# Experts' rows written back by token, and read in plain loads, in a windowed-attention, banded-attention and expert block

## Time and profile before

| | us |
|---|---|
| median of three runs | 3094.0 |
| lowest and highest | 3090.27 and 3098.82 |
| span of the profiled execution, first to last instruction | 3088.7 |
| PE busy | 2544.2 |
| DVE busy | 1965.5 |
| ACT busy | 1865.7 |
| POOL busy | 1914.2 |

### The profile page before, as it was taken

How to read it: one execution, slowest core, us unless ns; L and a number is a source line. 1 busy time by engine, 2 the same in 40 slices (tenths; PEclk the granted TensorE clock), 3 DMA queues, 4 the chain that set the end, 5 groups by cost and what they waited for, 6 DMA issues and landing times.

```text
span 3088.7 us, 77036 instructions
## 1 busy us (share of the span) xinstructions
PE 2544.2 (82%) x27338; PEld 1794.8 (58%) x27338; DVE 1965.5 (64%) x5091; ACT 1865.7 (60%) x3409; POOL 1914.2 (62%) x2270
## 2 busy tenths in 40 slices
PE   6898889989888899889988988899888887676830
PEld 3565655556666666666666666666665665554520
DVE  4577777777666666777676676767776765522222
ACT  3666656666767677677776677767777654432310
POOL 1335555555444444576666576666667878779986
PEclk9998888888999999899999999999999988788965
DMA  5223333334445454144333343434343434456743
GB/s 208 104 110 117 117 132 150 147 127 138 147 173 182 161 183 161 60 148 123 100 122 117 107 144 122 126 96 127 119 149 111 131 109 135 123 171 203 244 127 91
DMA packets 262427, 421.99 MB, mean 137 GB/s; under 512 B 41740, under 2 KB 141080, under 8 KB 261280
## 3 DMA queue, kind: packets, MB, share of 16 engines
q1 hardware_dynamic: 219232, 327.69, 31.2%
q0 software_dynamic: 32768, 67.17, 7.7%
q10 hardware_dynamic: 10048, 22.19, 2.2%
HBM read 198.26 MB, written 231.22 MB: 139 GB/s over the span
## 4 chain that ended last, share of the span: by engine, by line
PE 48%; POOL 17%; ACT 15%; issue 10%; DVE 7%; DMA 2%; ACTq 1%; SPq 1%; POOLq 0%; DVEq 0%
PE bank_m L834 7%; POOL yg L1233 7%; PE bank_m L827 4%; PE bank_to L761 4%; POOL x_sorted L1223 4%; PE bank_s L801 4%; PE bank_s L807 3%; PE bank_s L716 3%; ACT pt_sb_a L1051 2%; POOL xin L1243 2%; PE bank_to L770 2%; PE bank_s L729 2%; ACT L1178 2%; ACT v_a L1036 2%; PE bank_s L739 2%
## 5 line engine op out<-in xcount | busy, mean ns | idle before, releaser
L1223 POOL DMA_INDIRECT x_sorted<-xn_c,place_i x512 | 534.3, 1044 | 282.1 <-PE bank_s L700 109.2
L1233 POOL DMA_INDIRECT yg<-y_sorted,place_i x512 | 521.4, 1018 | 241.1 <-PE bank_to L783 107.5
L1216 POOL TENSOR_TENSOR s_sb_a<-s_sb_a,mx_a 128x512 f32<-128x512 f32 x256 | 267.8, 1046 | 587.7 <-DVE mx_a L1607 586.9
L1599 DVE TENSOR_TENSOR s_sb_a<-bank_s,bias_a 128x512 f32<-128x512 f32 x256 | 176.6, 690 | 355.3 <-PE bank_s L700 257.7
L827 PE MATMUL bank_m<-xe,wk_e 128*128 128x512 f32 x552 | 280.5, 634 | 37.7 <-ACT hid L1084 27.7
L834 PE MATMUL bank_m<-wk_e,hid 128*128 128x128 f32 x2208 | 283.3, 291 | 0.9 <-ACT hid L1084 0.9
L834 PEld LDWEIGHTS bank_m<-wk_e,hid 128*128 128x128 f32 x2208 | 277.7, 208 | 2.2 <-issue 1.9
L1216 POOL TENSOR_TENSOR s_sb_b<-s_sb_b,mx_b 128x512 f32<-128x512 f32 x256 | 269.7, 1054 | 11.5 <-DVE mx_b L1607 11.5
L761 PE MATMUL bank_to<-k_consts,p_sb_b 128*128 128x128 f32 x1024 | 179.0, 300 | 92.2 <-ACT pt_sb_a L1051 56.1
L1051 ACT ACTIVATE pt_sb_b<-bank_to 128x512 f32<-128x512 f32 x256 | 152.5, 596 | 146.4 <-PE bank_to L761 145.7
L1207 POOL TENSOR_TENSOR km_a<-qk_a,k_consts 128x128 f32<-128x128 f32 x512 | 215.7, 445 | 40.0 <-DVE qk_a L1451 35.4
(11 more groups left out here) (221 smaller groups left out, 6266.7 us busy)
## 6 DMA issues: line engine op xcount, KB each, us to landing
y_sorted<-t_back SPq DMA_DIRECT2D x192, 512.0 KB, 5.5
y_sorted<-yo SPq DMA_DIRECT2D x170, 256.0 KB
wk_e<-in_w_experts_dram SPq DMA_DIRECT2D x134, 321.0 KB
xs<-x_sorted SPq DMA_DIRECT2D x134, 256.0 KB
t_kept<-t SPq DMA_DIRECT2D x64, 256.0 KB
t_back<-t_kept SPq DMA_DIRECT2D x32, 512.0 KB
xin<-in_x_dram SPq DMA_DIRECT2D x128, 112.0 KB
x_res<-in_x_dram SPq DMA_DIRECT2D x256, 56.0 KB
```

The source lines that it names most:

```text
L1216: pool.tensor_tensor(s[:, :, :], s[:, :, :], m[:, :, None].to_broadcast(shape), ALU.subtract).then_inc(s_sub[w], 1)
L1223: pool.indirect_dma_start(out=x_sorted[group_of[d] % XSIDES].ap(), out_offset=bass.IndirectOffsetOnAxis(ap=place_i[:, d, n:n + 1], axis=0) ...
L1233: pool.indirect_dma_start(out=yg[:, c % 2, n, :], out_offset=None, in_=y_sorted[side].ap(), in_offset=bass.IndirectOffsetOnAxis(ap=place_i ...
L1599: tt(s_sb[0][:, :, :].rearrange("p (r h) n -> p r (h n)", h=2), scores, bias_a[:, kind, :, :].rearrange("p (r h) n -> p r (h n)", h=2), AL ...
```

## The change

**What it does.** Each row that is scattered to `x_sorted` is 130 floats wide now: 128 channels, the row of the output that belongs to the token (`HOME`), and the token's first expert (`FIRST`). When a tile comes back, DVE works out from these two, and from the number of the tile's own expert, which row each output belongs to (`back_to`), and POOL scatters the tile by it to `y_tokens`, with 4 indirect DMAs of 128 rows for each tile (`scatter_back`). The two outputs of a token lie side by side there, so an image's 2048 rows are contiguous, and SP loads them with one plain DMA of 1 MB (in `bring_back`). So `store_pair`, `gather`, `fill` and `apart` are gone, and `scatter_back` is new on POOL. `yo` has three buffers.

The places of the indirect DMAs are written out in two lists, as (step, move place), with steps from 8 on in the next pass: `BACK_AT` for the 8 of each slot's pair, `OUT_AT` for the 16 of an image. A second image is summed in passes 24 to 26 and 29 to 31. For the images of the tail there are four buffers for outputs and residuals, laid over buffers that only the passes need. Several small buffers share memory now, and the constants are split into two inputs.

```diff
-PAUSE = 4
-YSIDES = 3
-UNPAUSED = 4
-FILLS = BUFFER // TOKENS
-FILLS_PER_PASS = 12
+PART = 1
+HOME, FIRST, ROW_W = D, D + 1, D + 2
+YO, MOVES = 3, PART * SUB
+BACK_AT = (((4, 1), (4, 1), (4, 2), (4, 3), (4, 3), (5, 0), (5, 1), (5, 2)),
+           ((6, 1), (6, 2), (6, 3), (7, 1), (7, 2), (7, 3), (8, 0), (8, 1)),
+           ((9, 1), (9, 2), (9, 3), (10, 1), (10, 2), (11, 0), (11, 1), (11, 2)))
+OUT_AT = ((5, 0), (5, 2), (5, 3), (6, 0), (6, 1), (6, 2), (6, 3), (7, 0), (7, 1), (7, 2), (7, 3),
+          (8, 0), (8, 1), (8, 2), (8, 2), (8, 3))
-TWO_SUMS_FROM = 29
-PAIRS_PER_SUM = 2.5
+TWO_SUMS_FROM = 24
+PAIRS_TO_SUM = 3
...
             def bring_back(c):
...
+                sp.dma_start(t2_home[kept].rearrange("p t d -> p (t d)"), t2_kept.ap()[c, :, :]).then_inc(t2_in[kept], 16)
+                after(sp, stored[home], 16 * IO_DMAS * y_uses(c))
+                tiles_landed(sp, last_tile[group_of[c]])
+                first = last_image[group_of[c] - 1] + 1 if group_of[c] else 0
+                at = TOP * (SPARE + TOKENS * (c - first))
+                rows = y_tokens[group_of[c]].ap()[at:at + TOP * TOKENS, :]
+                sp.dma_start(y_home[home].rearrange("p t n d -> p (t n d)"),
+                             rows.rearrange("(p r) d -> p (r d)", p=P)).then_inc(y_in[home], 16)
...
-            def gather(c, n):
-                done, side = last_tile[group_of[c]], group_of[c] % YSIDES
...
+            def scatter_back(u, k):
+
+                _, q, _ = pairs[u].members[k // MOVES]
+                if k % MOVES == 0:
+                    pool.wait_ge(yo_ready, q + 1)
+                j = k % MOVES
+                pool.indirect_dma_start(out=y_tokens[pairs[u].group].ap(),
+                                        out_offset=bass.IndirectOffsetOnAxis(ap=back_to[:, q % YO, j:j + 1], axis=0),
+                                        in_=yo[:, q % YO, j, :], in_offset=None).then_inc(y_out[q % YO], 16)
...
                 def moves(k):
 
+                    for j in (i - 1, i):
+                        at = (t + TILES * (i - j), k)
+                        for slot in range(SLOTS_PER_PASS):
+                            u = slots[j][slot] if 0 <= j < PASSES else None
+                            if u is not None:
+                                for m, when in enumerate(BACK_AT[slot][0:MOVES * len(pairs[u].members)]):
+                                    if when == at:
+                                        scatter_back(u, m)
+                        if on(j - 3):
+                            for row, when in enumerate(OUT_AT):
+                                if when == at:
+                                    scatter(j - 3, row)
...
-            for c in range(first_tail_sum, IMAGES):
-                for k in range(TOP * TILES):
-                    gather(c, k)
-                    if c < IMAGES - UNPAUSED:
-                        apart()
+            for row, (t, _) in enumerate(OUT_AT):
+                if t >= TILES:
+                    scatter(IMAGES - 1, row)
+            for u in tail:
+                for k in range(MOVES * len(pairs[u].members)):
+                    scatter_back(u, k)
...
             def slots_back(q, m, banks):
...
-                after(dve, y_out[q % 2], 16 * (q // 2))
-                tt(yo[:, q % 2, :, :], banks[:, m, :].rearrange("p (j d) -> p j d", j=SUB),
-                   w[:, None, B2_AT:B2_AT + D].to_broadcast([P, SUB, D]), ALU.add).then_inc(yo_ready, 1)
+                after(dve, y_out[q % YO], 16 * MOVES * (q // YO))
+                for h in range(PART):
+                    stt(back_to[:, q % YO, SUB * h:SUB * h + SUB], rows[:, h, :, FIRST], w[:, h, OWN_AT:OWN_AT + 1],
+                        rows[:, h, :, HOME], ALU.not_equal, ALU.add)
+                tt(yo[:, q % YO, :, :].rearrange("p (n j) d -> p n j d", n=PART),
+                   banks[:, m, :].rearrange("p (n j d) -> p n j d", n=PART, j=SUB),
+                   w[:, :, None, B2_AT:B2_AT + D].to_broadcast([P, PART, SUB, D]), ALU.add).then_inc(yo_ready, 1)
```

More of the change, by code:

```diff
@@ L119, in shape_constants @@
     put("base", rows(REGION * e))
+    put("experts", rows(e))
+    put("home", TOP * (SPARE + TILES * ch[:, None] + np.arange(TILES)[None]))
     img = np.zeros((SIDE, SIDE), np.int32)
@@ L576, in _ @@
                     store_image(s)
-                if here[0] is not None:
-                    store_pair(here[0])
                 if first:
@@ L584, in _ @@
                     load_residual(a, 0)
-                if here[1] is not None:
-                    store_pair(here[1])
-                if i >= 0:
-                    for n in range(FILLS_PER_PASS * i, min(FILLS_PER_PASS * (i + 1), YSIDES * FILLS)):
-                        fill(n)
                 following = slots[i + 1][0] if i + 1 < PASSES else None
@@ L826, in hidden @@
                         pe.wait_ge(gelu_ready, CH * q + ch - 1)
-                    mm(banks[:, ch, :], w[:, P * ch:P * ch + P], xe[:, m, :], start=True, stop=True).then_inc(z_ready, 1)
+                    for h in range(PART):
+                        own = slice(SLOTS * h, SLOTS * h + SLOTS)
+                        last = mm(banks[:, ch, own], w[:, h, P * ch:P * ch + P], xe[:, m, own], start=True, stop=True)
+                    last.then_inc(z_ready, 1)
             def expert_out(q, m, end, banks):
@@ L1083, in gelu @@
                     act.wait_ge(z_ready, CH * q + ch + 1)
-                    func(hid[:, CH * m + ch, :], banks[:, ch, :], ACT.Gelu,
-                         bias=w[:, B1_AT + ch:B1_AT + ch + 1]).then_inc(gelu_ready, 1)
+                    for h in range(PART):
+                        own = slice(SLOTS * h, SLOTS * h + SLOTS)
+                        last = func(hid[:, CH * m + ch, own], banks[:, ch, own], ACT.Gelu,
+                                    bias=w[:, h, B1_AT + ch:B1_AT + ch + 1])
+                    last.then_inc(gelu_ready, 1)
             act.preload_act_table_set(EXP_LN_SET)
@@ L1300, in _ @@
                     step(i, t)
-            for k in range(12, TOP * TILES):
-                scatter(IMAGES - 1, k)
-                apart()
-            for c in sums[PASSES - 1][1:]:
-                for k in range(12, TOP * TILES):
-                    gather(c, k)
-                    apart()
-            for c in range(first_tail_sum, IMAGES):
-                for k in range(TOP * TILES):
-                    gather(c, k)
-                    if c < IMAGES - UNPAUSED:
-                        apart()
+            for row, (t, _) in enumerate(OUT_AT):
[4 more added lines that the diff above has]
+                    scatter_back(u, k)
         @block.vector
@@ L1592, in biased @@
+                    tt(rows[:, :, 0, :], rows[:, :, 0, :], t2_home[kept], ALU.add).then_inc(summed, 1)
             def biased(w, n):
```

330 lines of the change are left out of this document (155 added, 175 removed).

## The result

The changed kernel takes 3140.3 us (median of four runs, 3139.3 to 3150.1), the kernel before 3092.1 us beside it. The ratio is 1.0172, with a 95% interval of 1.0129 to 1.0215: 1.7% slower, where 1.1% was forecast. The profiled execution has a span of 3137.6 us; the forecast had 3121.7.

What follows compares the result with a forecast made beforehand. PE was the busiest engine, with POOL's masking holding it up in crowded passes and POOL's gathers setting the end. Span 3088.7 + 97 - 64 = 3121.7 us, plus 5.3 to the median: 3127 us, 1.1% slower; 8 in 10 range 3035 to 3168.

Steps and rivals of the forecast that it cites:

- The passes lose, the tail gains: Whole kernel: pass 33's step 4 comes 97 us later, and the tail from there takes 64 us less.
- the rival in which the passes take the moves in their stride: Passes: PE's late start is partly caught up, 2.5 us lost a pass, 3048 us in all; chance 0.31.
- A crowded step is POOL's: Passes: POOL needs 2.6 + 1.27 n us for a step of n moves, 11.5 in step 6, 12.8 in step 7.
- PE is late, and the light steps don't make it good: Passes without a sum: PE waits for POOL's masked keys and can't catch up; 4.6 us a pass, 32 for seven.
- A sum meets the masking: Nine passes summing an image: DVE's product at step 5 meets POOL's masking; 7.8 us a pass, 70 in all.
- The full clash: Rival: each pass with a sum loses 9.9 us, 3159; with every fourth tail move at 1.91 us, 3209; chance 0.09.
- Passes 17 and 23: No pair in the first slot, so step 4 is light: 5.5 us lost in each, 11 us together.
- The last passes: Passes 29 and 30 become 92.3 us each, -5 together; pass 31 gains 3 us, pass 32 gains 8.
- The tail: From pass 33's step 4, POOL's moves are the bound: 318 us where it was 382, -64 us.
- At nothing: Fills, SP's stores, 1 MB loads and DVE's additions cost or gain nothing; additions, if uncovered, 30 us in all.

Runs made afterwards that it cites:

- e1_out: Changed kernel with one list altered: an image's 16 scatters go out in steps 5 to 7, 0 and 1 instead of 5 to 7 and 0; 3013.9 us.
- e9_behind: Changed kernel, same moves in each step, but in steps 6, 7 and 0 those between subtractions and masking stand behind the masking; 3064.4 us.
- e7_late: Changed kernel with a single sum at step 1 of the next pass instead of at steps 5 and 6; 3108.6 us.
- e8_fills: Changed kernel with the 192 stores of 512 KB of zeros put back into passes 0 to 15; 3142.0 us.
- e12_no_rows: Changed kernel without DVE's computation of the rows: indices filled once ahead of the first pass, scatters and places kept; 3170.7 us.
- e3_home: Changed kernel with DVE's computation of the rows replaced by one operation filling indices from a constant, scatters and places kept; 3135.6 us.

## Why the prediction was right, point by point

- *The passes lose, the tail gains.* By step 4 of pass 33 the kernel is 121.3 us behind where 97 were forecast, and the tail takes 309.7 us where 318 were. Both parts have their sign and nearly their size; the rival in which the passes take the moves in their stride is out, and e1_out shows that it takes one list to make it true.
- *A crowded step is POOL's.* Forecast 11.5 and 12.8 us for the steps 6 and 7, measured 12.26 and 12.85. The 0.8 us more are masking at 1.29 for 0.76 us and a move of 1.25 us, both in step 6. The two subtractions and the masking are 2.86 us by the prediction's own figures and not 2.6; gaps of 0.16 us instead of 0.30 between a move and another operation make up for it.
- *PE is late, and the light steps don't make it good.* Shown by PE's waits of 2.60 and 2.40 us and by e9_behind. Mis-sized is the loss of a pass without a sum: the seven lost 43.0 us together, not 32, 6.1 us each and not 4.6. The clock had been left out, and it is about half of what these passes lost (12.7 of 23.7 us in the passes 11 to 14). What lowers it is not shown: in e1_out step 1 has 0.70 too, without such a wait.
- *A sum meets the masking.* Forecast 7.8 us a pass, measured 82.8 / 9 = 9.2. The 3.2 us put down to the sum were right in size (94.5 for 91.2, and e7_late takes 3.4 away), but not in place: the prediction had the product meet step 5's masking, and that masking ends before the product begins. The product holds up a move, and the additions hold up step 6's masking and the move behind it: 1.4, 1.0 and 0.8 us in pass 20. That the sum comes out at the forecast's is in part luck. What made such a pass longer than forecast is the crowding beneath. The Trainium skill, "SBUF — State Buffer", section "SBUF: two separate sides", made an estimated 9.4 us of such a pass. The measured 9.2 is nearer to it, but not for its reason: it had 4.8 us for the sum, and the sum added 3 to 3.4; no run here shows that POOL was shut out for a whole sum.
- *The full clash* as a rival had 9.9 us for such a pass and was nearly met there, but by the crowding and not by the sum; in the tail it had every fourth move long, and 9 of 201 were.
- *Passes 17 and 23.* Forecast 5.5 us each, measured 8.1 and 13.3. This step failed: no pair in the first slot lightens step 4, but the steps 6 and 7 are as full as in other passes (14.0 and 12.9 us in pass 17, 14.0 and 13.3 in pass 23).
- *The last passes.* 29 and 30 became 95.3 and 98.0 us, not 92.3. Of this, 1.4 us each is what all passes with a sum took over the forecast; the other 1.6 and 4.3 stay open. The second image that they sum does not explain them: the steps 1 and 2, where its sum stands, take 24.2 and 24.1 us together, and 24.1 and 23.9 in the passes 19 and 21, which sum one. 31 and 32 gave back 28 us and not 11. For 31 the prediction misread the kernel before: it had the pauses begin behind that stretch, but the first stands at 2578.2, and 25 of them lie inside (2536.3 to 2626.1). PE's need, from which it took 87 us, was no bound either: PE is busy for 63.9 of the 78.4 us. For 32, 41 moves, seven subtractions and the gaps fit into 64.0 us, since the waits that were put at 13 us are 5.
- *The tail.* It has 201 moves, not 208; at 1.264 us they are 254 us (forecast: 264). Nine long moves add 15.7 (forecast: 20); three waits for tiles add 13, which were not forecast; from the last move's end to the span's are 25.5 us (forecast: 34), because DVE waited 4.8 us for the first of the three last images, and the other two landed beside the sums. The forecast had all three loaded first, 21 us at the tail's mean of 213 GB/s; from 3116 to 3125 us the DMA engines moved 423.
- *At nothing.* The fills, by e8_fills; DVE's additions, though they took 0.68 us on average where the forecast had 0.2, by e12_no_rows, which leaves them out and is not faster.

The crowded passes took 35 us more than forecast and the passes 29 and 30 took 9 more; against that stand 17 us in 31 and 32, 8 in the tail and 2 ahead of pass 10. That some 16 us are left is luck: the signs and the main mechanism were right, and several terms were off by more than the whole.

The first pause of the kernel before, in POOL's timeline:

```profile
2578.25 0.55 POOL L1243 MEMSET xin<- 128x512 f32 x1
```

## What to carry to other kernels

Count a strictly ordered engine's work by step, not by pass: here forty moves fit into a pass without a sum at no loss, and cost 6 us, 9 with a sum, when two steps hold fifteen of them. What another engine waits for goes ahead of what nobody waits for; here that cost nothing with spread steps and gained with crowded ones. When a change removes pauses or transfers, ask of each stage alone whether that engine is its bound: the same engine was it in the tail, and was not in the passes until the lists made it so.

## What the runs showed of the hardware

- An indirect DMA's issue on POOL of 0.96 us took 1.89 to 3.07 us beside DVE's product, once for each of the nine sums in the tail that had moves beside them. The Trainium skill, "SBUF — State Buffer", section "A bandwidth-pool intuition that's wrong (but worth ruling out)", tells of a DMA of 620 ns that takes 3100 ns beside a DVE copy; the trace goes the same way, with a product of two tensors.
- Work is held up both ways, and short work of DVE too: 0.22 us became 2.69 us beside a move and two subtractions of POOL. With one tensor as input (e3_home) it was 0.15 to 2.74 us, so the number of inputs did not decide.
- The same matmuls took PE 128.5, 117.7 or 115.3 us in the passes 7 and 8, at a mean granted clock of 0.88, 0.96 or 0.98; the first two had the same places of POOL's moves. Where the moves stood made a difference over six passes (421 to 429 us against 405 to 414). Why one pass keeps the upper level in a step and the next doesn't stays open.
